# A fused two-layer recurrent network on one core: a program of its own for the last batch row

## What is computed

```python
x = x + s * silu(g)                      # layer 0: wavelet attention s, deep feed-forward g
xn = layernorm(x)                        # layer 1 begins
# recurrent block: selective scan over positions, 16 states per feature
h = exp(delta * A) * h + delta * Bm * xn ; y = sum_n(h * Cm) ; ssm = xn + y + D * xn'
block = gelu(layernorm(ssm) @ W1.T + b1) @ W2.T + b2 + ssm          # dense layer, 256 -> 1024 -> 256
# experts: 8 experts, 2 chosen per position
nf = (rms_norm(xc)).astype(bf16) ; logits = nf @ gate.T ; w = softmax(top2(logits))
g = min(p1_even, 7) ; lin = clip(p1_odd, -7, 7)                     # p1 = nf @ mlp1[e]
moe = xc + sum_e w_e * ((g * sigmoid(1.702 g) * (lin + 1)) @ mlp2[e])
out = x + block * silu(moe)
```

## Time and profile before

| what | value |
|---|---|
| median of 3 runs | 2015.63 us (2011.28 to 2016.68) |
| the profiled execution, device time | 2013.38 us |
| its span, first to last instruction | 2011.6 us |
| mean granted TensorE clock | 0.885 |
| PE / DVE / ACT / POOL busy over the span | 74% / 74% / 54% / 45% |
| share of the chain that ended last: PE, DVE, ACT, issue, POOL | 37%, 25%, 15%, 14%, 8% |

### The profile page before, as it was taken

How to read it: one execution, slowest core, us unless ns; L and a number is a source line. 1 busy time by engine, 2 the same in 40 slices (tenths; PEclk the granted TensorE clock), 3 DMA queues, 4 the chain that set the end, 5 groups by cost and what they waited for, 6 DMA issues and landing times.

```text
span 2011.6 us, 16362 instructions
## 1 busy us (share of the span) xinstructions
PE 1495.5 (74%) x5296; PEld 634.4 (32%) x5296; DVE 1498.2 (74%) x1796; ACT 1093.7 (54%) x1481; POOL 900.1 (45%) x578
## 2 busy tenths in 40 slices
PE   5898888688887777788878758878888743336975
PEld 1443433334432223333433223333433211002421
DVE  2663388799588868888678959878867879995294
ACT  3556677565535567666526567676525543333353
POOL 3141344535038853545008754544305774442097
PEclk8999999899989889899999889989998875557998
DMA  7000000001001000000100000000100010001000
GB/s 177 1 32 22 11 1 0 21 0 63 11 0 32 21 21 0 22 1 0 73 0 32 22 21 1 0 22 0 63 11 0 11 42 0 21 0 63 0 1 21
DMA packets 12599, 42.42 MB, mean 21 GB/s; under 512 B 1866, under 2 KB 1890, under 8 KB 10466
## 3 DMA queue, kind: packets, MB, share of 16 engines
q1 hardware_dynamic: 11698, 35.08, 4.8%
q0 software_dynamic: 816, 6.30, 1.4%
HBM read 38.23 MB, written 4.19 MB: 21 GB/s over the span
## 4 chain that ended last, share of the span: by engine, by line
PE 37%; DVE 25%; ACT 15%; issue 14%; POOL 8%; DMA 0%; POOLq 0%; SPq 0%; DVEq 0%; ACTq 0%
PE psf L1230 8%; PE psf L1221 6%; PE psu L1393 4%; PE psy L1381 4%; ACT da L907 3%; DVE st L1872 3%; POOL ap L675 3%; POOL gate L670 3%; DVE psu L1857 2%; PE psf L1143 2%; PE psu L1470 2%; ACT L795 2%; PE psy L1200 2%; PE psf L1200 2%; ACT L907 2%
## 5 line engine op out<-in xcount | busy, mean ns | idle before, releaser
L652 POOL TENSOR_TENSOR gx<-gx,sy 128x1024 f32<-128x1024 f32 x120 | 303.5, 2529 | 226.5 <-DVE sy L1886 226.5
L670 POOL TENSOR_TENSOR gate<-gate,lin 128x512 f32<-128x512 f32 x128 | 173.1, 1352 | 439.6 <-DVE lin L1990 438.6
L1470 PE MATMUL psu<-ap,mw 128*128 128x512 f16 x512 | 150.0, 423 | 91.3 <-POOL ap L675 91.3
L907 ACT ACTIVATE da<-delta,aneg 128x512 f32<-128x512 f32 x256 | 164.2, 710 | 82.2 <-DVE st L1872 49.3
L1857 DVE TENSOR_TENSOR psu<-so,psu 128x1024 f32<-128x1024 f32 x128 | 156.6, 1223 | 44.2 <-PE psu L1343 43.8
L643 POOL TENSOR_TENSOR g2p<-tf,g2p 128x512 fp32r<-128x512 f32 x64 | 85.9, 1346 | 225.0 <-ACT g2p L826 224.9
L1230 PE MATMUL psf<-g1p,h2w 128*128 128x512 f16 x768 | 177.7, 379 | 4.9 <-ACT tf L803 4.9
L1230 PE MATMUL psf<-hp,h1w 128*128 128x512 f16 x768 | 176.0, 379 | 5.9 <-ACT tf L795 5.9
L979 ACT ACTIVATE gate<-gate 128x512 f32<-128x512 f32 x128 | 80.4, 628 | 176.1 <-DVE gate L1979 175.9
L1886 DVE TENSOR_TENSOR sy<-st,psu 128x1024 f32<-128x1024 f32 x128 | 156.0, 1219 | 6.2 <-DVE st L1872 2.4
L1872 DVE TENSOR_TENSOR_SCAN st<-da,carry,psu 128x512 f32<-128x512 f32 x128 | 156.8, 1267 | 1.9
(11 more groups left out here) (314 smaller groups left out, 3086.6 us busy)
## 6 DMA issues: line engine op xcount, KB each, us to landing
mw<-in_mlp_w SPq DMA_DIRECT2D x4, 2048.0 KB, 8.1
wf<-in_wf SPq DMA_DIRECT2D x5, 1024.0 KB, 4.7
xn<-in_x SPq DMA_DIRECT2D x8, 512.0 KB, 6.4
xr<-in_x SPq DMA_DIRECT2D x8, 512.0 KB, 3.7
x<-gx SPq DMA_DIRECT2D x8, 512.0 KB, 3.8
mw<-in_mlp_w SPq DMA_DIRECT2D x4, 1024.0 KB, 10.1
out<-outc SPq DMA_DIRECT2D x8, 512.0 KB, 3.2
h1w<-in_h POOLq DMA_DIRECT2D x1, 2048.0 KB, 13.5
```

The lines of the kernel that those rows point to most:

```text
L652: pool.tensor_tensor(out, chunk(gx, c), sy[:, n % 2], ALU.add).then_inc(y_acc.sem, 1)
L670: pool.tensor_tensor(gate[:, r % NG], gate[:, r % NG], lin[r % NL][:], ALU.mult)\
L907: last = act.activation(da[:, n % 4, t], delta[c][:, t], ACT.Exp, scale=aneg[:, t, n:n + 1])
L1470: last = pe.matmul(psb[:, h], mw2[:, e, t, h * P:(h + 1) * P], ap2[r % NA][:, part], start=False, stop=(q == NQ - 1 and part == 1))
```

## The change

`batch(None, 3)` becomes `closing(3)`, with its own order on all four engines. Chunk 0's expert norm and gate go into the first seven steps of its own scan; its 16 expert quarters into steps 8 to 15, two per step. Chunk 1's scan then carries chunk 1's gate (steps 1 to 7) and chunk 0's dense layer (steps 6 to 15). What is left after the scan is the experts and the dense layer of chunk 1, interleaved. The gate chain runs once for each chunk on half the blocks, with scan instructions between its steps. The head of chunk 1 moves up to steps 1 to 10.

Layer 0's weights are dead by then, and their memory becomes a region: the last row's copies of the dense layer's first weights (`wf1_z`), of the experts' (`mw1_z`, `mw2_z`) and some buffers lie there, loaded once (`load_tail`) behind row 3's residual loads. `expert_up` uses only psy in the last row, each half waiting for the clip of the quarter before; `expert_down` of chunk 0 uses psf; `hidden1` of chunk 1 has one bank.

```diff
+        w1 = weights("w1", 0, [P, KD, F], F16)
+        mw1_z = weights("mw1_z", 8192, [P, E, KD, 2, D], BF16)
+        mw2_z = weights("mw2_z", 24576, [P, E, KD, D], BF16)
+        wf1_z = weights("wf1_z", 40960, [P, KD, F], F32)
...
+        def up_bank(b, r):
+            return psy if tail(b) or r % 2 == 0 else psg
+        def down_bank(b):
+            return psf if tail(b) else psb
+        def first_bank(b, c, m):
+            return psg[:, 1] if tail(b) and c == 1 else psy[:, m % 2]
+        def blocks(b, part):
+            half = NJ // NC
+            return slice(part * half, (part + 1) * half) if tail(b) else slice(0, NJ)
...
+        def expert_pair(n):
+            return (2 * (n - 8), 2 * (n - 8) + 1) if n >= 8 else ()
...
+            def load_tail(b):
+                sp.wait_ge(w3_mm.sem, w3_mm.at(b, NC * KF))
+                sp.dma_start(wf1_z[:], a["wf1"]).then_inc(wf1_z_in, 16)
+                sp.dma_start(mw1_z[:], a["mlp1_w"]).then_inc(mw_z_in, 16)
+                sp.dma_start(mw2_z[:], a["mlp2_w"]).then_inc(mw_z_in, 16)
...
-            load_hidden(B - 1)
-            load_experts(B - 1)
```

GpSimd's program of the last row:

```diff
+            def closing(b):
+                for n in range(NS):
+                    for r in expert_pair(n):
+                        expert_product(b, r)
+                        if r >= 1:
+                            expert_low(b, r - 1)
+                    state_add(b, 0, n)
+                expert_low(b, NQ - 1)
+                for n in range(NS):
+                    state_add(b, 1, n)
+                gated_out(b, 0, b)
+                expert_out(b, 0)
+                for r in range(NQ, Q):
+                    expert_product(b, r)
+                    if r > NQ:
+                        expert_low(b, r - 1)
```

ScalarE's:

```diff
+            def closing(b):
+                decay(b, 0)
+                decay(b, 1)
+                expert_square(b, 0)
+                for n in range(NS):
...
+                    for at, piece, c in ((1, head_square, 1), (1, expert_root, 0), (3, head_root, 1), (5, head_b16, 1),
+                                         (7, softplus, 1)):
...
+                    for r in expert_pair(n):
+                        expert_silu(b, r)
+                        if r >= 1:
+                            expert_high(b, r - 1)
...
+                expert_high(b, NQ - 1)
+                for n in range(NS):
+                    if n % 2 == 0 and n + 2 < NS:
+                        decay(b, NS + n + 2)
+                        decay(b, NS + n + 3)
+                    if n == 0:
+                        carry_state(b, NS - 1)
+                        expert_square(b, 1)
+                    if n == 1:
+                        expert_root(b, 1)
...
+                for i in range(NQ + 1):
+                    if i < NQ:
+                        expert_silu(b, NQ + i)
+                    if i >= 1:
+                        expert_high(b, NQ + i - 1)
+                    if i == 1:
+                        lf_square(b, 1, False)
+                    if i == 3:
+                        lf_root(b, 1)
+                    if 5 <= i < 5 + KF:
+                        hidden1(b, 1, i - 5)
```

TensorE's, and the waits of `expert_up`:

```diff
+                w, x = (mw1_z, nf_z) if tail(b) else (mw1, nf)
                 for half in range(2):
+                    if tail(b):
+                        pe.wait_ge(*((gmin_done.sem, gmin_done.at(b, r)) if half == 0 else
+                                     (lin_done.sem, lin_done.at(b, r))))
...
+            def closing(b):
+                spread_b(b, 0, 0)
+                for n in range(NS):
+                    spread_c(b, 0, n)
+                    pair = expert_pair(n)
+                    if pair:
+                        expert_up(b, pair[0], b)
+                        for r in (pair[0] - 3, pair[0] - 2):
+                            if r >= 0:
+                                expert_down(b, r)
+                    if n + 1 < NS:
+                        spread_b(b, 0, n + 1)
+                    if pair:
+                        expert_up(b, pair[1], b)
+                        if n + 1 < NS:
+                            expert_spread(b, n - 7, b)
+                    for at, piece, c in ((0, head_mean, 1), (0, expert_mean, 0), (2, head_var, 1), (2, expert_logits, 0),
+                                         (4, head_delta0, 1), (5, head_delta1, 1), (5, expert_turn, 0), (6, head_bc, 1)):
+                        if n == at:
+                            piece(b, c)
...
+                    if 6 <= n < 6 + KF:
+                        hidden1(b, 0, n - 6, False)
+                    if 7 <= n < 7 + KF:
+                        hidden2(b, 0, n - 7)
+                for i in range(NQ + 3):
+                    if i < NQ:
+                        expert_up(b, NQ + i, b)
+                    if i == 0:
+                        lf_average(b, 1, False)
+                    if i % KD == KD - 1 and 1 <= i // KD + 1 < E:
+                        expert_spread(b, E + i // KD + 1, b)
+                    if i == 2:
+                        lf_variance(b, 1)
+                    if i >= 3:
+                        expert_down(b, NQ + i - 3)
+                    if 5 <= i < 5 + KF:
+                        hidden1(b, 1, i - 5, False)
+                    if 6 <= i < 6 + KF:
+                        hidden2(b, 1, i - 6)
```

VectorE's:

```diff
+            def closing(b):
...
+                for n in range(3):
+                    state_step(0, n)
+                    if n == 1:
+                        head_center(b, 1)
+                expert_norm(b, 0)
+                state_input(b, 0, 3)
+                expert_choice(b, 0, beside_gate(0, ((2, state_scan, 3), (6, state_output, 3), (10, state_input, 4))))
+                state_scan(b, 0, 4)
+                state_output(b, 0, 4)
+                head_norm(b, 1)
+                head_norm1(b, 1)
+                state_input(b, 0, 5)
+                expert_weights(b, 0, beside_gate(0, ((14, state_scan, 5), (18, state_output, 5), (22, state_input, 6))))
+                state_scan(b, 0, 6)
+                head_z0(b, 1)
+                state_output(b, 0, 6)
+                state_input(b, 0, 7)
+                head_z1(b, 1)
+                state_scan(b, 0, 7)
+                expert_parts(b, 0)
+                state_output(b, 0, 7)
+                for n in range(8, NS):
+                    early, late = expert_pair(n)
+                    state_input(b, 0, n)
+                    expert_clip(b, early)
+                    state_scan(b, 0, n)
+                    expert_scale(b, early)
+                    state_output(b, 0, n)
+                    expert_clip(b, late)
+                    expert_scale(b, late)
+                    for at, piece in ((8, head_parts), (9, head_softplus), (10, head_late)):
+                        if n == at:
+                            piece(b, 1)
...
+                block_out(b, 0)
+                for i in range(NQ):
+                    expert_clip(b, NQ + i)
+                    expert_scale(b, NQ + i)
+                    if i == 0:
+                        lf_center(b, 1)
+                    if i == 4:
+                        lf_scale(b, 1)
+                block_out(b, 1)
+                expert_sum(b, 1)
```

More of the change, by code:

```diff
@@ L1469, in expert_down @@
                     for part in range(2):
-                        last = pe.matmul(psb[:, h], mw2[:, e, t, h * P:(h + 1) * P], ap2[r % NA][:, part],
+                        last = pe.matmul(out[:, h], w[:, e, t, h * P:(h + 1) * P], ap2_at(b, r)[:, part],
                                          start=False, stop=(q == NQ - 1 and part == 1))
@@ L1588, in batch @@
                                     piece(b0 + 1, 0)
+            def closing(b):
[17 more added lines that the diff above has]
+                        if n == at:
+                            piece(b, c)
+                    if n == 7:
+                        expert_spread(b, 0, b)
+                spread_b(b, 1, 0)
+                for n in range(NS):
+                    spread_c(b, 1, n)
+                    for r in {0: (13,), 1: (14, 15)}.get(n, ()):
+                        expert_down(b, r)
+                    if n + 1 < NS:
+                        spread_b(b, 1, n + 1)
+                    for at, piece, c in ((0, expert_mean, 1), (3, lf_variance, 0), (2, expert_logits, 1),
+                                         (6, expert_turn, 1)):
+                        if n == at:
+                            piece(b, c)
+                    if n == 1:
+                        lf_average(b, 0, False)
+                    if n == 8:
+                        expert_spread(b, E, b)
+                    if 6 <= n < 6 + KF:
+                        hidden1(b, 0, n - 6, False)
[16 more added lines that the diff above has]
+                        hidden2(b, 1, i - 6)
@@ new lines, in expert_weights, with last8 @@
+            def expert_weights(b, part=0, beside=None):
+                step = gate_steps(b, part * GATE_STEPS + CHOICE_STEPS, beside)
```

(19 more changed lines are left out.)

314 lines of the change are left out of this document (214 added, 100 removed).

## The result

The changed kernel took 2025.36 us (median of 13 runs, 2017.84 to 2030.4), the kernel before 2013.02 in 13 runs beside it: ratio 1.0053, 95% interval 1.0039 to 1.0066. It is slower by half a per cent; the interval says 8 to 13 us. The profiled execution has a span of 2021.7 us, 10.1 more than the one of before.

A forecast was written before the change was run, and what follows sets the result against it. VectorE was taken to bound the scan, with a dense phase and GpSimd-heavy experts after it. Chunk 0's scan +64, chunk 1's +23 and the stretch behind them -77 made +10 us: 2025.6, range 2003 to 2040.

The forecast's parts named there:

- both scan terms: Last row: S (first state_input) to V (chunk 1's first) +64 us; V to T (last state_output's end) +23.
- the saving behind T: From the last state_output's end (T) to the kernel's end: 103.5 us against 180.6, so -77.
- Port waits of the small steps: Both scans: small gate steps beside GpSimd's add wait 2.35 us each, the upper bound; 9.4 for both chunks.
- no-change rival: Both scans: the gate's small steps don't wait for GpSimd; -9.4 us, so +0.6 and 2016.2; chance 0.15.
- The gate's steps, 6.5 per chunk: Both scans: the gate adds 26 VectorE steps at 0.25 us, 6.5 per chunk.
- Early clip waits, 5 x 1.75: Chunk 0's scan, steps 11 to 15: the early clip waits for expert_up behind expert_spread, 1.75 us each, 8.8 together.
- Output 6 and 7, 4.5 and 1.2: Chunk 0's scan: output 6 waits for spread_c behind head_delta1, 4.5 us; head_bc before output 7 costs 1.2.
- The carry, 4.9: Chunk 1's first scan waits for carry_state(15), which lies behind expert_high(15) on ScalarE: 4.9 us.
- Behind T, the start: After the last state_output, up to the end of quarter 22's up: 33.5 us; 8.6 shorter at full TensorE clock.
- Odd quarters, 7.6: After the scans: in odd quarters expert_spread waits for its own quarter's scale, so nothing hides: 7.6 us each.
- My rival for the clock's fall: After the scans: idling in odd quarters lowers TensorE's clock, up to 2.6 us four times; +20, 2035.6; chance 0.15.
- Faster rival: Chunk 0's steps 5 to 15 and after the scans: TensorE gets 2.4 GHz, -19 us, so 2006.6; chance 0.22.

The follow-up runs named there:

- all five: Changed kernel with both spreads later, carry_state before expert_high(15), large gate steps behind a scan, head_delta1 and head_bc later: 1981.39 us, ratio 0.9827.
- the last of the reordered kernels: Changed kernel with all five, plus the dense layer's norm earlier and chunk 1's expert_mean behind its second spread_c: 1977.17 us, ratio 0.9806.

## Why the prediction was right, by its steps

The total was 2025.6, the median is 2025.36. That is closer than the account deserves. From S to the end the change costs +6.0 us in the profiled executions where I had +10: both scan terms were too high, the saving behind T too large, and 4.2 us before S, which belong to no term, filled the gap. The base moved as well: the median of before was 2015.63 in the three runs I had and 2013.02 in thirteen, so median to median the change costs 12.3. Even the interval's 8 to 13 us lie above the 6.0 that my terms are about. Only one execution of the kernel before was profiled, so where the other 2 us and more come from stays open. That the sum hit the median is luck.

- **VectorE bounds the scan**: shown. Removing waits shortened S to V from 157.5 to 141.9 with VectorE's work falling only from 140.0 to 135.9.
- **Port waits of the small steps**, taken at the upper bound: right. Four steps took 2.33, two per chunk, and moving them gave 7.3 back. The norm's, 2.0 and 2.35, came to 2.0 each. The no-change rival, on which the small steps would have been free, falls.
- **The gate's steps, 6.5 per chunk**: the step of the sum that was mis-sized in the scans. Steps 3 to 6 of chunk 1 are 12.4 longer than 4 x 4.88, of which 4.07 is `lf_scale`; the gate with both port waits is 8.3, not 11.2. A 32-column step takes 0.22 from start to start, a four-column one 0.18 to 0.21, only the last few of 64 columns up to 0.25, and the step before a scan or product partly fills a start gap. This explains 2.9 of the 3.2 missing in V to T, and by the same count some 2.5 in S to V (8.7 in place of 11.2).
- **Early clip waits, 5 x 1.75**: the mechanism right, the count high. Steps 11 to 15 wait 0, 1.76, 0.50, 1.77, 1.76, together 5.8 in place of 8.8. Step 11 was counted wrongly: `head_late`, 4.4 us at the end of step 10, lies ahead of its early clip, and its up had ended 4 us before that clip. In step 13 TensorE had its full clock. That is 3.0 of the 6 missing in S to V. The norm's and the logits' latency, put at 1.8, showed as waits of 0.57 and 0.30.
- **Output 6 and 7, 4.5 and 1.2**: 4.79 and 0.93. **The carry, 4.9**: 5.03; but its removal is worth 1.9 alone. The term described this order rightly; as a price of the step it would have been wrong.
- **Head parts**: 7.07 from cast to next clip against 7.3.
- **Behind T, the start**: quarter 22's up ends, and its clip starts, at T + 33.8, against 33.5, but two misses offset one another on the way. I had TensorE at low clock up to quarter 21; from the spread ahead of `up` 18 on (1923.31) it had full clock, and the clips of quarters 19 and 21 came at T + 14.3 and 25.2, not 17.3 and 27.7. Then it idled for 6.26 us before quarter 21's spread, and `expert_down` and the first `hidden1` ran at low clock (1.91 and 3.20), where I had full.
- **Odd quarters, 7.6**: the step that failed. They took 9.67, 9.67 and 7.97. With full clock 7.97, 0.4 more than I had; with low clock 1.70 more. Even ones took 5.16. Quarters 22 to 28 are 47.9 against 43.4, quarter 29 is 6.26 against 5.8, the rest 20.8 as forecast: +5 in all. My rival for the clock's fall gave it 2.6 four times; it came twice, at 1.7. It was a partly true rival, not a separate case. Its source, shows four f16 matmuls, not bf16 ones as I wrote, in one place only; the low clock did not follow every such gap.
- **Faster rival** (full clock all along): falls. The clock was 0.71 and 0.76 in the scans and 0.86 behind T, and of the 19 us that full clock was to bring, the 1.25 of step 13 came and, for a while, some 3 in the start, which were lost again by quarter 22.
- **Loads**: cost nothing, as said.
- **Up to S**: +4.2 where the two programs are the same. The last section tells what it is. It helped the sum to come out.

That effects of waits add was not in the forecast; it is what all five showed.

## What to carry to other kernels

Mixing two phases saves their unused engine time only if the order on the narrowest queue is made anew: here the same overlap cost 12 us as written and, in the last of the reordered kernels, saved 36. Look for an instruction that waits for data just being made and has independent work queued behind it (`expert_spread` ahead of 4.3 us of matmuls). Put small operations that read only SBUF where GpSimd is idle: here 0.2 us of work cost 2.3 beside its add. And price an idle stretch of TensorE twice: for the wait, and for the low clock that may follow, here 1.3 to 1.7 us each time it did.

## What the hardware showed that I had not expected

The 4.2 us before S come largely from one instruction (4.7 longer, of which 3.4 are left at the same product of the next row). In the pipeline over rows stands a product with both inputs in SBUF, at the end of a clip and scale, while GpSimd works through a queue without gaps. Timelines of VectorE and GpSimd, the kernel before:

```profile
1086.93 1.48 DVE L1784 TENSOR_TENSOR y<-y,rsb 128x1024 f32<-128x1024 f32 x1
...
1084.98 2.35 POOL L664 TENSOR_TENSOR gx<-gx,xr 128x1024 f32<-128x1024 f32 x1
1087.29 2.25 POOL L670 TENSOR_TENSOR gate<-gate,lin 128x512 f32<-128x512 f32 x1
```

and the changed one:

```profile
1087.64 6.16 DVE L2037 TENSOR_TENSOR y<-y,rsb 128x1024 f32<-128x1024 f32 x1
...
1085.66 2.38 POOL L741 TENSOR_TENSOR gx<-gx,xr 128x1024 f32<-128x1024 f32 x1
1087.97 1.30 POOL L747 TENSOR_TENSOR gate<-gate,lin 128x512 f32<-128x512 f32 x1
1089.19 1.20 POOL L752 TENSOR_TENSOR ap<-gate,ap 128x512 f16<-128x512 f32 x1
1090.31 1.30 POOL L747 TENSOR_TENSOR gate<-gate,lin 128x512 f32<-128x512 f32 x1
1091.54 1.18 POOL L752 TENSOR_TENSOR ap<-gate,ap 128x512 f16<-128x512 f32 x1
```

Either VectorE gets in after one add (1.48 us, and GpSimd's next product takes 2.25 in place of 1.27), or it stands aside for the add and four more instructions until GpSimd's queue runs out, 6.16. I had expected a wait of one instruction at most. Over the ten profiled executions of this study, whose programs are the same there, the chunk-1 product of rows 1, 2 and 3 (with the same neighbours) took 1.5 in 15 of 30 cases and 5.6 to 6.2 in the others, with no pattern by kernel. What it costs can be read off in rows 1 and 2, from this product to chunk 0's product of the next row: 450.1 to 450.2 us where it took 1.5, 452.9 where it took 5.6, and 453.5 to 453.6 where it took 6.2, in all twenty cases. So each hold costs the row 2.8 to 3.5 us, and three rows can differ by 10. S lay between 1646.0 and 1653.5 in the ten executions, at 1648.1 in the kernel before, so the 4.2 are not a price of the change; the number of holds does not account for all of that spread, though. What tips it stays open: the product starts 1.95 us behind the add's start in the kernel before (1.48 long), 1.95 in the run with the spread behind the early up (6.16 long) and 1.98 here (6.16 long).

The second surprise is how little separates the clock's levels: three odd quarters with the same matmuls and the same idle time of 2.44 us, two followed by 1.2 GHz for 3 us and one by full clock, and, in another execution of the same order, all three by full clock. Nor does the fall come at one place: in quarter 23 `expert_down` behind the idle stretch still took 1.02 us and `hidden1` then 3.46, in quarter 25 `expert_down` already took 1.92.
